# A windowed attention loop on four engines: the rotation behind the projection, the squares behind the value copies

## What is computed

```python
def _layer(x, wqkv, qs, ksc, wo, lg, lb, w1, b1, w2, b2):      # x: 2 x 1024 x 128, 8 heads of 64
    h = shift_token(x)                                         # half the channels one token later
    q, k, v = jnp.split(h @ wqkv, 3, axis=-1)
    q, k, v = (to_heads(q), to_heads(k), to_heads(v))
    q = l2norm(q) * qs
    k = l2norm(k) * ksc
    q, k = rotary_xpos(q, k)                                   # q * cos * scale + rotate_half(q) * sin * scale
    o = local_attention(q, k, v)                               # windows of 64, each sees itself and the one before
    x = x + o.transpose(0, 2, 1, 3).reshape(b, n, INNER) @ wo
    h = layernorm(shift_token(x)) * lg + lb
    a, g = jnp.split(h @ w1 + b1, 2, axis=-1)
    return x + (a * gelu(g)) @ w2 + b2

for l in range(2):
    x = _layer(x, ...)
```

## Time and profile before

| | us |
|---|---|
| median of 3 runs | 1512.34 |
| lowest and highest | 1511.67, 1512.66 |
| the profiled execution | 1508.53 |
| its span, first to last instruction | 1506.5 |
| TensorE busy | 1333.5 |
| VectorE busy | 1013.3 |
| ScalarE busy | 792.7 |
| GpSimd busy | 361.6 |

### The profile page before, as it was taken

One profiled execution on the slowest core, in us unless ns is written; L12 is line 12 of the kernel. 1 busy time (PEld: TensorE's weight loads), 2 busy tenths in 40 slices (PEclk: granted clock), 3 DMA queues, 4 the chain that ended last, 5 costly groups with the idle time before them and its releaser, 6 DMA issues.

```text
span 1506.5 us, 23829 instructions
## 1 busy us (share of the span) xinstructions
PE 1333.5 (89%) x9009; PEld 790.8 (52%) x9009; DVE 1013.3 (67%) x2202; ACT 792.7 (53%) x1681; POOL 361.6 (24%) x288
## 2 busy tenths in 40 slices
PE   6999999999999999999589999987279988799886
PEld 4767677776777673333223333333146654366652
DVE  5767767687766856765577667740967775877755
ACT  4544435444444442434136666675169984499851
POOL 0000000011000003335410000000267771477732
PEclk9999999999999999999569999999589999999998
DMA  5000000000000000002023111100200000000000
GB/s 141 1 1 1 1 1 1 1 1 1 1 1 1 0 1 1 1 0 81 29 77 82 46 37 37 36 3 7 57 1 2 2 2 1 1 2 2 2 1 28
DMA packets 23725, 26.03 MB, mean 17 GB/s; under 512 B 5602, under 2 KB 20140, under 8 KB 22316
## 3 DMA queue, kind: packets, MB, share of 16 engines
q1 hardware_dynamic: 23612, 24.51, 5.5%
HBM read 20.11 MB, written 4.39 MB: 16 GB/s over the span
## 4 chain that ended last, share of the span: by engine, by line
PE 64%; ACT 14%; DVE 13%; issue 4%; POOL 2%; DMA 2%; SPq 0%; POOLq 0%; DVEq 0%; ACTq 0%
PE ps L679 13%; PE ps L699 8%; PE ps L714 7%; ACT probsT L2283 6%; PE ps L1051 4%; PE ps L1010 4%; PE ps L1031 3%; DVE negmax L1437 2%; PE ps L888 2%; PE ps L882 2%; PE ps L1182 2%; PE ps L650 2%; ACT v_st L2253 2%; PE ps L1173 2%; PE ps L872 2%
## 5 line engine op out<-in xcount | busy, mean ns | idle before, releaser
L2208 ACT ACTIVATE probsT<-ps 128x512 f32<-128x512 f32 (+1 forms) x304 | 163.6, 576 | 103.7 <-PE ps L1035 91.6
L1437 DVE TENSOR_REDUCE negmax<-ps 128x1 f32<-128x1024 f32 x128 | 150.7, 1219 | 72.5 <-PE ps L699 72.4
L2030 ACT ACTIVATE probs<-ps,negmax 128x1024 f32<-128x1024 f32 x128 | 142.5, 1114 | 80.5 <-DVE negmax L1437 76.5
L2036 ACT COPY probsT<-ps 128x512 f32<-128x512 f32 x128 | 74.8, 584 | 168.2 <-PE ps L714 168.1
L714 PEld LDWEIGHTS ps<-ident,probs 128*128 128x128 f32 x1024 | 114.5, 141 | 66.2 <-issue 44.0
L714 PE MATMUL ps<-ident,probs 128*128 128x128 f32 x1024 | 138.4, 277 | 6.6 <-DVE probsT L1450 3.4
L2360 POOL TENSOR_SCALAR rstd<-mv 128x4 f32<-128x4 f32 (+1 forms) x23 | 5.3, 233 | 578.5 <-DVE mv L1372 578.4
L1010 PE MATMUL ps<-arena 76*128 76x512 bf16 (+3 forms) x384 | 113.6, 355 | 26.4 <-DVE cmax L1705 20.6
L699 PE MATMUL ps<-k_st,q_st 64*128 64x512 f32 x512 | 128.7, 622 | 5.9 <-ACT probs L2030 5.9
L1705 DVE CUSTOM_DVE_ANT_0 k_st<-ps,rel 128x256 f32<-128x256 f32 (+7 forms) x128 | 96.8, 756 | 44.1 <-PE ps L1010 43.2
L1705 DVE CUSTOM_DVE_ANT_0 q_st<-ps,rel 128x256 f32<-128x256 f32 (+7 forms) x128 | 96.7, 756 | 41.9 <-PE ps L1010 41.0
(11 more groups left out here) (245 smaller groups left out, 2565.1 us busy)
## 6 DMA issues: line engine op xcount, KB each, us to landing
arena<-c_parts SPq DMA_DIRECT2D x32, 192.0 KB
arena<-c_parts SPq DMA_DIRECT2D x16, 128.0 KB
arena<-in_L_ffn_w_dram SPq DMA_DIRECT2D x3, 512.0 KB
c_parts<-probsT SPq DMA_DIRECT2D x2, 768.0 KB, 3.5
arena<-in_c_far_dram SPq DMA_DIRECT2D x16, 96.0 KB
c_parts<-work SPq DMA_DIRECT2D x2, 768.0 KB, 11.3
work<-in_L_ffn_wqkv_dram SPq DMA_DIRECT2D x1, 1536.0 KB
x_sb<-in_L_attn_x_dram SPq DMA_DIRECT2D x2, 512.0 KB, 5.9
```

The lines of the kernel that those rows point to most:

```text
L1437: dve.tensor_reduce(negmax[:, u:u + 1], s2, AX_X, ALU.max, negate=True).then_inc(s_a_negmax, 1)
L2030: act.activation(probs[:, u % NPB, :], s2, ACT.Exp, bias=negmax[:, u:u + 1], accum_out=rowsum[:, u:u + 1]).then_inc(s_a_exp, 1)
L2208: act.activation(c_p[:, kt % 2, j0:j0 + heads, q0 - kt * P:q0 - kt * P + n], ps[:, 4 + c % 2, 0:heads * n].rearrange("p (h n) -> p h n", n ...
```

## The change

Four things are done to the two attention loops, all else stays:

- Squares. In ScalarE's step the square of tile t + 3 behind the exponentials becomes that of tile t + 2, behind the value copies and ahead of the copy of transposed weights. It waits for the rotation of its tile (s_d_m), no longer for the projection; the rotation waits for the projection (s_d_qkp), no longer for the square.
- Rotation. VectorE rotates tile t + 3 near the end of step t, where it rotated t + 2 at its start. The reciprocal of step t stands between the two parts of the rotation. The key addition follows at once, and the norms of t + 2 stand ahead of the rotation.
- GpSimd. Of the next tile's work, the power and the key product now come directly behind the product with the reciprocals, and the query addition last, for tile t + 3.
- Old values. The copy of the older values into d_vs is now VectorE's last work in a step, one step later than the values that it reads, with a semaphore of its own, s_d_vs. TensorE waits for it before the weighted values, ScalarE before it overwrites the older buffer.

Ahead of both layers the preparation is put in the same order; in the second the rotation of tile 2 stands ahead of the last shift and the tables. The diff without the declaration of s_d_vs:

```diff
@@ -1199,6 +1200,8 @@
             pe.wait_ge(s_d_pT, n)
+            if exists(t, -2):
+                pe.wait_ge(s_d_vs, n)
             pe.wait_ge(s_d_v, n)
@@ -1764,7 +1767,7 @@
 
-def rotate(l, t):
+def rotate(l, t, between=None):
         n, par = TILES * l + t, t % 2
@@ -1774,10 +1777,12 @@
 
-        dve.wait_ge(s_d_sq, n + 1)
+        dve.wait_ge(s_d_qkp, n + 1)
         if exists(t, -2):
...
         dve.tensor_tensor(mA, qk, heads(rot_c[:, t:t + 1, :, :]), ALU.mult)
+        if between:
+            between()
         for d, e in ((0, 32), (32, 0)):
@@ -1785,12 +1790,15 @@
         n, par = TILES * l + t, t % 2
+        if exists(t, -2):
+            dve.wait_ge(s_d_qkt, n - 1)
         dve.wait_ge(s_d_m, n + 1)
...
         n, par = TILES * l + t, t % 2
+        dve.wait_ge(s_d_sq, n + 1)
         dve.tensor_reduce(ss[:, par, :], d_sq[:, par, :].rearrange("p (h d) -> p h d", d=HD2),
@@ -1799,8 +1807,13 @@
         n, par = TILES * l + t, t % 2
-        if exists(t, 2):
-            rotate(l, t + 2)
+        def inverse():
+            dve.wait_ge(s_d_e, n + 1)
+            dve.reciprocal(d_rr[:, par, :], d_sum[:, par, :]).then_inc(s_d_rr, 1)
+        if t == 0:
+            add_keys(l, 2)
         if exists(t, 0):
@@ -1814,19 +1827,28 @@
                .then_inc(s_d_pT, 1)
-        if exists(t, 2):
-            add_keys(l, t + 2)
-            norms(l, t + 2)
         if exists(t, -2):
...
             dve.tensor_tensor(z, ps[:, 3, 0:P], z, ALU.add).then_inc(s_d_z, 1)
+        if exists(t, 2):
+            norms(l, t + 2)
         if piece:
             piece()
+        if exists(t, 3):
+            rotate(l, t + 3, inverse)
+            add_keys(l, t + 3)
+        elif exists(t, 0):
+            inverse()
         if exists(t, 0):
-            dve.wait_ge(s_d_e, n + 1)
-            dve.reciprocal(d_rr[:, par, :], d_sum[:, par, :]).then_inc(s_d_rr, 1)
+            if exists(t, -1):
+                dve.wait_ge(s_d_v, n)
+                if exists(t, -2):
+                    dve.wait_ge(s_d_o, n - 1)
+                dve.tensor_copy(d_vs[WIN:P, par, :], d_va[WIN:P, 1 - par, :]).then_inc(s_d_vs, 1)
+            else:
+                dve.sem_inc(s_d_vs, 1)
 
@@ -1887,6 +1909,7 @@
 norms(0, 1)
+rotate(0, 2)
 for l in range(DEPTH):
@@ -1936,9 +1959,9 @@
         add_keys(l + 1, 0)
-        norms(l + 1, 0)
     gated(l, 10)
     if not last:
+        norms(l + 1, 0)
         next_shift(l, 1)
@@ -1956,6 +1979,7 @@
         next_shift(l, 2)
+        rotate(l + 1, 2)
         next_shift(l, 3)
@@ -2249,7 +2273,7 @@
             act.wait_ge(s_d_ss, n - 1)
-        act.wait_ge(s_d_qkp, n + 1)
+        act.wait_ge(s_d_m, n + 1)
         act.activation(d_sq[:, par, :], ps[:, 0:2, :].rearrange("p n c -> p (n c)"), ACT.Square)\
@@ -2267,12 +2291,13 @@
         if exists(t, 0):
+            act.wait_ge(s_d_vp, n + 1)
             if exists(t, -1):
-                act.wait_ge(s_d_v, n)
-                act.copy(d_vs[WIN:P, par, :], d_va[WIN:P, 1 - par, :])
-            act.wait_ge(s_d_vp, n + 1)
+                act.wait_ge(s_d_vs, n)
             act.copy(d_va[:, par, :], ps[:, 3, :])
             act.copy(d_vs[0:WIN, par, :], ps[0:WIN, 3, :]).then_inc(s_d_v, 1)
+        if exists(t, 2):
+            square(l, t + 2)
         if exists(t, -1):
@@ -2285,8 +2310,6 @@
             ins.then_inc(s_d_e, 1)
-        if exists(t, 3):
-            square(l, t + 3)
 
@@ -2307,7 +2330,7 @@
     if l == 0:
-        for t in range(3):
+        for t in range(2):
             square(l, t)
@@ -2328,12 +2351,11 @@
         if l + 1 < DEPTH:
-            if j == 8:
+            if j == 9:
                 square(l + 1, 0)
...
         act.activation(tpre[:, 1:2], eps_c[:, 0:1], ACT.Exp)
-        square(l + 1, 2)
 
@@ -2477,33 +2499,47 @@
 
-def unit_norm(l, t):
+def add_queries(l, t):
 
...
         pool.wait_ge(s_d_m, n + 1)
+        if exists(t, -2):
+            pool.wait_ge(s_d_qkt, n - 1)
         pool.tensor_tensor(kq[:, 0:INNER], d_mA[:, par, 0:INNER], d_mB[:, par, 0:INNER], ALU.add)\
             .then_inc(s_d_add, 1)
+def unit_norm(l, t):
+        n, par = TILES * l + t, t % 2
         pool.wait_ge(s_d_cl, n + 1)
...
         pool.wait_ge(s_d_addk, n + 1)
+        pool.wait_ge(s_d_add, n + 1)
         pool.wait_ge(s_d_rn, n + 1)
-        v = kq[:, INNER:2 * INNER].rearrange("p (h d) -> p h d", d=HD2)
+        v = d_kq[par][:, INNER:2 * INNER].rearrange("p (h d) -> p h d", d=HD2)
         pool.tensor_tensor(v, v, d_rn[:, par, H2:2 * H2].unsqueeze(2).to_broadcast([P, H2, HD2]), ALU.mult)\
...
         n, par = TILES * l + t, t % 2
-        if exists(t, 0):
-            v = d_p[:, par, :, :]
-            pool.wait_ge(s_d_rr, n + 1)
-            pool.tensor_tensor(v, v, d_rr[:, par, :].unsqueeze(2).to_broadcast([P, H2, P]), ALU.mult)\
-                .then_inc(s_d_p, 1)
+        v = d_p[:, par, :, :]
+        pool.wait_ge(s_d_rr, n + 1)
+        pool.tensor_tensor(v, v, d_rr[:, par, :].unsqueeze(2).to_broadcast([P, H2, P]), ALU.mult)\
+            .then_inc(s_d_p, 1)
         if exists(t, 2):
             unit_norm(l, t + 2)
-unit_norm(0, 0)
-unit_norm(0, 1)
+        if exists(t, 3):
+            add_queries(l, t + 3)
+def begin(l):
+    add_queries(l, 0)
+    unit_norm(l, 0)
+    add_queries(l, 1)
+    unit_norm(l, 1)
+    add_queries(l, 2)
+begin(0)
 for l in range(DEPTH):
@@ -2513,8 +2549,7 @@
     if l + 1 < DEPTH:
-        unit_norm(l + 1, 0)
-        unit_norm(l + 1, 1)
+        begin(l + 1)
 for c in range(NCH):
```

More of the change, by code:

```diff
@@ L424, in build @@
         s_d_addk = sem("s_d_addk")
+        s_d_vs = sem("s_d_vs")
         s_d_s = sem("s_d_s")
```

## The result

The changed kernel takes 1517.11 us, median of 14 runs (1515.06 to 1519.18); the kernel before took 1511.72 in 14 runs beside it. The ratio is 1.0035, 95% interval 1.0027 to 1.0043: 5.4 us slower. The forecast was 1512.8, no measurable change. By its own measure of 3 us for a change that can be told from none, this is the case "slower", to which it gave 0.27. Its range of 1503 to 1519 held the time, but its likeliest case, 1509.5 to 1516.5, did not: the time lies in the part that the range owes to rival B, which is not what happened. The step in the loop came out as worked out, 9.27 us for 9.24. Most of the miss lies where the loops end, above all between tile 13 and tile 14.

What follows compares the result with a forecast made beforehand. ScalarE's order, not its sum, was taken to bound the 9.04 us step. 22 steps +4.4, starts -1.4 and -1.7, ends -0.8 sum to +0.5 us: 1512.8 us against a median of 1512.34, range 1503 to 1519.

Steps and rivals of the forecast that it cites:

- slower: Whole kernel slower by more than about 3.0 us; chance 0.27, from rivals B, C and some 7 per cent of the likeliest case.
- likeliest case: Key addition in the loop held by GpSimd's product, step 9.24 us; 1512.8 us, own range 1509.5 to 1516.5; chance 65%.
- rival B: In the loop the old-value copy loses a turn to GpSimd's power: step 9.5 us, 1518.5 us in all; chance 18%.
- Today's bound: Loop step of 9.04 us bound by ScalarE's order, not its sum; the square costs 0.90 us where TensorE waits.
- The floor: TensorE's own ring in a loop step: 6.46 + 1.07 + 1.18 = 8.71 us, so 0.33 of the square's 0.90 can be had.
- The new ring: Loop: exponentials, reciprocal, key addition held by GpSimd's product, old-value copy, value copies, square, exponentials; 9.24 us, +4.4 over 22 steps.
- Tile 13 to 14: Step near the loops' end stays near 9.5 us: loses an addition (0.60), gets its start later by about as much.
- GpSimd's order "costs nothing": In the loop, power first and query addition last cost nothing; keys are ready some 2 us before TensorE transposes them.
- Starts: Start of the attention loops: first layer -1.4 us, or -0.9 if TensorE's clock falls; second layer -1.7 us.
- Rival D: Both layers' starts give nothing because TensorE's clock falls: +2 to +4 on the forecast; counted in its spread, no own chance.
- rival C: In the loop GpSimd's power holds the old-value copy for its whole length: step about 12 us, 1574 us; chance 2%.
- Rival A: In the loop the key addition is not held by GpSimd's product: step 8.71 us, 1501 us in all; chance 15%.

## Why the prediction was right and wrong

- *Today's bound, and what the square is worth.* Right. The floor was put at 8.71; five kernels, in which the held addition and the copy do not stand together in the ring, run at 8.76 or 8.77.
- *The new ring and the held addition.* Right: 9.24 forecast, 9.27 measured, addition 1.26, copy 0.42. Shown by taking the copy out of the ring in two ways and the addition in a third (8.77 each), and by making GpSimd hold the copy as well (10.24). The first of the eleven steps takes 9.68 in both layers, which the walk did not have; over both layers 5.8 us instead of 4.4.
- *Tile 13 to 14.* The step that failed. It was put at "near 9.5 us", its chain losing an addition and starting later by as much. It takes 10.69, 1.17 more than before. The forecast's two terms came: the maximum starts 0.58 later after the scores, and the addition's 0.60 is gone, so they cancel. Two more were missing: VectorE waits 0.40 for the output product, and the clip is held 0.70. The clip's hold is borne out by the run with the query addition first; the other is read from the timeline alone. I had followed the key addition through its collision and not asked what else VectorE would now have under GpSimd's moved query addition. Twice 1.17 is the largest single part of the miss.
- *GpSimd's order "costs nothing".* True for when the keys are ready, false for VectorE between tile 13 and 14, for the reason just given.
- *Starts.* The first is right in size (-1.2 for -1.4) with one premise not borne out: behind a gap of 2.73 us the granted clock was 0.50 all the same. The second start and the first layer's end gave -1.1 and -1.5 instead of -2.1. There the gap of TensorE is 6.96 us and the scores run at the lower clock, as forecast, but the tables, after two collisions, let the maximum start at 1308.84, 6.9 us after tile 0's scores, where it was 6.5 before. Rival D, that the starts give nothing if the clock falls in both, is out too: it fell in both, and they gave 1.2 and about 1.3 us.
- *The power, rivals B and C.* The Trainium skill (SBUF — State Buffer, Who interferes with whom) has the shared ports held for a whole instruction, also by a copy in two-port mode. The trace agrees for GpSimd's additions and products, and the held copy (1.07) and clip (0.87) are of its kind. It does not agree for the power: the copy ran at 0.42 from 1140.74, under a power recorded from 1140.12 to 1143.48. So rival C did not come. Nor did rival B: the addition held the power's start (3.36 for 2.91), and the copy lost no turn. The step is 9.27 and not 10.24 because it is the power that waits behind the product; the query addition in its place holds the copy 0.97 us. The same section of the Trainium skill says that whoever issues first gets the ports. The trace agrees in the run with the copy behind the reciprocal, where the copy starts 0.04 us ahead of the product: copy 0.42, product 2.13 for 1.90.
- *Rival A* (the addition not held, 1501 us) is out by the addition's 1.26.
- *Small slips in the working,* which change nothing: the row of L1754 is a copy of 64 x 511, not 512; the row gives 0.47 us behind GpSimd's end where the sum has 0.48; and 22 steps cost 3 us more than starts and ends give from a step of 9.35 on, not 9.37.

In sum: 22 steps cost 1.4 more than forecast, tile 13 to 14 2.3 more, and starts and ends gave about 0.6 less. That is 4.3 of the 4.9 us between +0.5 and +5.4. Tile 14 to 15, on which the forecast said nothing, took another 1.4 in the profiled executions, partly by the clock. The ring was right by its mechanism; that the range held the time owes something to its width.

## What to carry to other kernels

Look for the ring, not for the busy engine: a piece moved into an engine's idle time is free, a piece that another engine's ring must pass is not, and a copy of 0.42 us cost 12 us by its place in a list. Where VectorE and GpSimd both work on SBUF, draw both lists side by side after a reorder and check every instruction for what it now lies under, small ones too. And try the parts of a change one by one: here one of four carried the whole gain in the loop.

## What the runs showed of the hardware

- A VectorE copy within SBUF of 64 x 512 with a single input is held by a GpSimd product (1.07 for 0.42) and by a GpSimd addition (1.39); a scalar operation on 128 x 16 too (0.87 for 0.17). A GpSimd power of 128 x 16, three microseconds long, held neither a copy (0.42) nor an addition (0.68) that started 0.26 us or more into it, but was itself held at its start by an addition (3.36 for 2.91).
- Held GpSimd instructions: the product by VectorE's copy (2.13 for 1.90), the query addition by VectorE's key addition (1.72 for 1.27).
- The same code with the same TensorE gap of 3.04 us was followed by a granted clock of 1.00 in one execution and 0.50 in another; the stretch took 10.89 and 12.47 us.
